# One of three weight subtractions of each expert moved from VectorE to GpSimd

## What is computed

```python
for e in range(E):
    a = _swiglu(xt @ expert_up_w[e].T)          # silu(gate half) * up half, I = 352
    out = out + cw[:, e:e + 1] * (a @ expert_down_w[e].T)
```

## Time and profile before

| | |
|---|---|
| time of the profiled execution | 2214.22 us |
| its span in the trace | 2212.1 us |
| TensorE busy, mean granted clock | 1779.5 us (80%), 0.901 |
| VectorE busy | 1611.7 us (73%) |
| ScalarE busy | 793.1 us (36%) |
| GpSimd busy | 1009.2 us (46%) |
| stage of the experts | from about 1700 us to the end |

### The profile page before, as it was taken

The page is one execution under the profiler, slowest core; times in us unless marked ns, Lnnn a source line. Parts: engine busy times, 40 slices in busy tenths (PEclk is TensorE's granted clock), DMA queues, the critical chain, the costliest instruction groups (busy, mean ns, idle before and its releaser), DMA issues. The chain is left out here.

```text
span 2212.1 us, 31372 instructions
## 1 busy us (share of the span) xinstructions
PE 1779.5 (80%) x8084; PEld 1285.4 (58%) x8084; DVE 1611.7 (73%) x2184; ACT 793.1 (36%) x1172; POOL 1009.2 (46%) x777
## 2 busy tenths in 40 slices
PE   3778767687676876768866668979997999999998
PEld 3345544454434554445543435657786999999997
DVE  0369999999989999899998834335763566655664
ACT  0444555445464553645545401211001233332332
POOL 1057547676576764767756532000001444433443
PEclk9989879798897997879978888999998999999999
DMA  5111101111101120011201042221121656666564
GB/s 135 69 29 64 53 25 35 39 58 56 29 30 40 54 64 24 30 40 49 69 25 30 24 162 85 95 106 57 58 79 44 163 124 165 162 146 164 143 161 82
DMA packets 81603, 169.61 MB, mean 77 GB/s; under 512 B 22459, under 2 KB 27467, under 8 KB 77979
## 3 DMA queue, kind: packets, MB, share of 16 engines
q1 hardware_dynamic: 57360, 116.06, 15.6%
q0 software_dynamic: 17856, 44.85, 10.4%
q10 hardware_dynamic: 6187, 6.37, 1.1%
HBM read 261.62 MB, written 39.24 MB: 136 GB/s over the span
## 5 line engine op out<-in xcount | busy, mean ns | idle before, releaser
L789 POOL TENSOR_TENSOR dbx<-u,b_all 128x512 f32<-128x512 f32 x512 | 642.2, 1278 | 350.5 <-DVE h L687 345.2
L687 DVE TENSOR_TENSOR_SCAN h<-da,dbx 128x512 f32<-128x512 f32 x512 | 596.2, 1203 | 40.2 <-ACT da L587 40.2
L587 ACT ACTIVATE da<-delta,a_neg 128x504 f32<-128x504 f32 x512 | 347.9, 684 | 474.1 <-DVE h L687 469.2
L427 PE MATMUL hT<-ident,h 128*128 128x128 f32 x2048 | 313.5, 313 | 229.6 <-DVE h L687 229.0
L427 PEld LDWEIGHTS hT<-ident,h 128*128 128x128 f32 x2048 | 274.8, 163 | 342.9 <-issue 337.6
L700 DVE SCALAR_TENSOR_TENSOR yacc<-hT,c_now,yacc 128x512 f32<-128x512 f32 x480 | 331.4, 732 | 4.3 <-PE hT L427 4.2
L334 PE MATMUL bank<-hid,w_in 128*128 128x512 f32 x608 | 291.4, 627 | 7.6 <-ACT hid L467 7.6
L1921 POOL DMA_INDIRECT out<-y,slots_kept x76 | 135.6, 1784 | 226.4 <-issue 158.1
L334 PEld LDWEIGHTS bank<-hid,w_in 128*128 128x128 f32 x608 | 120.4, 207 | 137.0 <-issue 128.1
L1554 POOL DMA_DIRECT2D slots_kept<-lists_kept x1 | 0.6, 577 | 331.2 <-DVE lists_kept L1508 331.2
L394 PE MATMUL bank<-w_out,skip 128*128 128x512 f32 x320 | 147.7, 609 | 2.5 <-DVE skip L659 2.5
(11 more groups left out here) (234 smaller groups left out, 3312.7 us busy)
## 6 DMA issues: line engine op xcount, KB each, us to landing
w_up_kept<-in_up_T SPq DMA_DIRECT2D x76, 1408.0 KB, 6.1
w_dn_kept<-in_dn_T SPq DMA_DIRECT2D x76, 768.0 KB, 7.4
b_all<-bt_scratch SPq DMA_DIRECT2D x128, 256.0 KB, 3.2
x_in<-in_x_pad ACTq DMA_DIRECT2D x21, 256.0 KB
res<-in_x_pad SPq DMA_DIRECT2D x20, 256.0 KB, 3.7
x_scratch<-res SPq DMA_DIRECT2D x20, 256.0 KB, 3.4
w_in<-in_in_T SPq DMA_DIRECT2D x8, 512.0 KB, 4.7
x_in<-x_scratch SPq DMA_DIRECT2D x4, 1024.0 KB, 5.3
```

Source lines behind the costliest of these rows:

```text
L427: mm = nc.tensor.transpose(hT[t][:, d * P:(d + 1) * P], h[:, m % RING, d, t * P:(t + 1) * P], ident[:])
L587: nc.scalar.activation(out[:, :, 1:], rows[:, :, 1:], ACT.Exp, scale=a_neg[:, d, n:n + 1]) \
L687: nc.vector.tensor_tensor_scan(h[:, n % RING, i, :], da[i % RING][:], dbx[:, i, :], 0.0, ALU.mult, ALU.add).then_inc(scan_done, 1)
L789: nc.gpsimd.tensor_tensor(dbx[:, i, :], u[:, d, :], b_all[:, m % RING, :], ALU.mult) \
```

## The change

The low part of the gate weights is no longer made by VectorE. A new function of GpSimd's program, `split_gate`, waits for `gate_split` and does the same subtraction of 128 x 1408 float32 numbers; it stands between the gather and the add of GpSimd's step i, when tile i starts a run. On VectorE the other two subtractions move up by one place each: `lower_up` takes the place of `lower_gate` ahead of `swiglu`, and `lower_down` the place of `lower_up` behind it; the extra look at the table for `lower_down` one step later goes away.

```diff
             first = weight_parts(dve, 0)
             x_out(0, 0)
-            lower_gate(first)
             lower_up(first)
             lower_down(first)
...
             with dve.If(run_starts):
-                lower_gate(parts)
+                lower_up(parts)
             swiglu(0, 0)
             with dve.If(run_starts):
-                lower_up(parts)
+                lower_down(parts)
...
                 x_out(i + 2, s)
-                started, of_started = starts(dve, i + 1), weight_parts(dve, i + 1)
-                with dve.If(started):
-                    lower_down(of_started)
                 with dve.If(run_starts):
-                    lower_gate(parts)
+                    lower_up(parts)
                 swiglu(i + 1, (r + 1) % RING)
                 with dve.If(run_starts):
-                    lower_up(parts)
+                    lower_down(parts)
...
+            def split_gate(i):
+
+                run = pool.value_load(table[0:1, 2, bass.ds(i, 1)], min_val=1, max_val=EXP)
+                slot = slot_of(run)
+                hi, lo = [part[:, slot, :, 0:INNER].rearrange("p o k f -> p (o k) f") for part in (w_up_hi, w_up_lo)]
+                pool.wait_ge(gate_split, run)
+                lo_part(nc.gpsimd, lo, w_up[:, :, 0:INNER], hi).then_inc(gate_ready, 1)
...
+            pool.sem_inc(gate_ready, 1)
...
                 gather(r % RING, ahead % LISTS, 16 * (j + loads), i + 1)
+                starts = pool.value_load(table[0:1, 1, bass.ds(i, 1)], min_val=0, max_val=1)
+                with pool.If(starts):
+                    split_gate(i)
                 add(i, r + TILES_AHEAD)
```

More of the change, by code:

```diff
@@ L1850, in a_out @@
                 less.then_inc(aT_out, 1)
[L1852 to L1855, removed]
             def lower_up(parts):
@@ L1872, in _ @@
             dve.sem_inc(aT_out, 1)
-            dve.sem_inc(gate_ready, 1)
             dve.sem_inc(up_ready, 1)
```

## The result

The changed kernel takes 2278.19 us (median of 4 runs, 2275.82 to 2281.9) against 2216.12 us (4 runs) of the kernel before: a ratio of 1.0279, 95% interval 1.0254 to 1.0303. The forecast was 2279 us. Over the later runs the kernel before has a median of 2216.89 us (28 runs, 2206 to 2225). The profiled execution of the changed kernel took 2278.81 us, with a span of 2276.7, 64.6 us more than before.

The account below looks back on a forecast made before the run. TensorE was taken to bound the experts' stage. Waits of 44.0 + 5 - 7.8 = 41 us plus 24 us of lowered clock made 65 us on 2214.22, so 2279 us; range 2230 to 2305 us.

Parts of the forecast that it names:

- What bounds the stage, and what could be won: Experts' stage: TensorE sets the time; all its waits after the stage's start, 7.8 us, are what relief for VectorE can return.
- The collision: Run starts: VectorE's up subtraction waits in full for GpSimd's, so swiglu and then TensorE come late, 2.9 us lost.
- When GpSimd can start: Run starts: GpSimd needs 1.2 us behind its gather for table and branch, bounds 0.3 and 1.83, starting at about 3.9.
- the second kind: 7 run starts with the gather ending at 3.4 to 4.7: VectorE goes first, go_up late, 2.4 us each, 16.8 us.
- The three kinds of starts: Experts' stage: the 15 run starts split into 6, 7 and 2 by when GpSimd's gather ends, together 44.0 us.
- the first kind: 6 run starts with the gather ending by 2.9: GpSimd goes first, 2.9 us lost each, 17.4 us.
- The first run: Start of the experts' stage: TensorE waits for GpSimd's gate part, 4.3 or 6.0 us later than before, taken as 5.
- The clock: Experts' stage: TensorE's standstills lower its granted clock 8.5 times at 2.8 us, 24 us, bounds 0 and 42.
- The clock doesn't stay: Judges the rival for the experts' stage that waits are the same but the clock stays: 2255 us, chance 0.18.
- Side by side: Rival at the run starts: GpSimd's and VectorE's subtractions run at the same time without hindrance; 2232 us, chance 0.10.
- GpSimd is last at every start: Rival at the run starts: slow table reading or growing lateness puts GpSimd behind VectorE each time; 2327 us, chance 0.12.
- the relief of VectorE could win: Rival in the experts' stage: moving lower_down wins 7.8 us and GpSimd's work is hidden; 2206 to 2210 us, chance 0.05.

Follow-up runs that it names:

- swiglu first: The changed kernel with VectorE's order at a run start turned to swiglu, then up part, then down part; 2227.12 us, ratio to before 1.0053.
- the run with filled standstills: The changed kernel with 14 extra matmuls on TensorE at each run start, ahead of the activation's transposes; 2252.08 us, ratio to before 1.0149.
- GpSimd relieved: The changed kernel with swiglu ahead of the up part and the down part one step later behind swiglu; 2227.22 us, ratio to before 1.0058.
- up part first: The changed kernel with GpSimd also waiting for VectorE's up part before it subtracts; 2290.89 us, ratio to before 1.0336.

## Why the prediction held, point by point

*What bounds the stage, and what could be won.* Right. TensorE without a wait takes 474.5 us; the waits were 7.6 to 7.8 us, all of them from the order on VectorE, and a version that moves one piece of VectorE's work takes them all back. The change's own move of the down part did too.

*The collision.* Right, and shown: VectorE's up part takes 3.39 us in the median beside a GpSimd subtraction, 1.63 beside a GpSimd instruction that only writes, 1.62 alone. It works in both directions: at tile 56 of the kernel with swiglu first, GpSimd's subtraction takes 4.20 us behind an up part that VectorE had begun 0.43 us before. That it reaches TensorE through `swiglu` was right as well: with `swiglu` ahead, 49 of the 56 us go.

*The price of the subtraction on GpSimd.* 3.2 us expected, 3.22 measured.

*When GpSimd can start.* Wrong. I took 1.2 us behind the gather for the table and the branch. At 12 of the 15 starts of the changed kernel the subtraction starts 0.25 us behind ScalarE's gate copy, so nothing of the table shows. Where the gather is what GpSimd waits for, it can start 0.02 us behind it (tile 41: gather to 3.52, subtraction from 3.54). At two starts there is more than either accounts for: at tile 15 it starts 0.81 us behind the gather and 0.46 behind the copy, at tile 56 0.19 and 0.41. With that, GpSimd is ready ahead of VectorE at many of the starts that I had put in the second kind.

*The three kinds of starts.* Wrong in their numbers: there was only the first kind, at all 15 starts. Besides the table's time, I had carried over GpSimd's lateness from the trace of before, but in the changed kernel the gather ended by 3.8 at all 15 starts, in place of up to 6.8. The sum was 44.0 us; what was measured is 40.2 us, as the 15 delays of the activation's transposes against 6.36 (9.04 on average), or 39.8 by the run with filled standstills. The two errors, dearer kinds and too many of them, came to 4 us only, since the kinds cost 2.4 and 4.9 us around the 2.9 of the first.

*The first run.* 5 us expected, 2.9 measured: GpSimd was ready at once there too, at 1712.3, 3.39 us behind the row transposes, and went ahead of both of VectorE's parts.

*The clock.* 24 us expected, 23.9 measured, but by other factors: it fell at 14 of the 15 starts, where I had 8.5, and a fall cost 1.7 us, where I had 2.8. That the two products agree is luck. The gaps were 2.1 to 3.0 us. I had counted on the scan stage, where gaps of 2.1 to 2.6 us lowered the clock half the time; here they did nearly always. And in the start at 2063 the clock was back by 2065.8 (the matmul spacing goes from 0.29 to 0.16 us there), while behind the gap at 1580 it took until 1589.

*The sum.* 65 us against 64.6 in the profiled execution looks closer than it is: 5.7 us of that are the launch's spread ahead of the stage, and the changed stage itself cost 58.8, that is 40.2 + 2.9 + 23.5 - 7.8. Against the median of before over all runs the difference is 61.3 us. The forecast was 6 us too high for the stage, and in the profiled execution the launch's spread happened to fill that up.

*The rivals.* The clock doesn't stay: the fill run would have shown no gain. Side by side is out by the stretched instructions. That GpSimd is last at every start didn't happen in the changed kernel, but forcing it gave the slowest kernel of all, 2290.89 us. That the relief of VectorE could win fails for a reason that I had named only in part: even with `swiglu` out of the collision's way (GpSimd relieved) the kernel is slower than before, since GpSimd's lateness behind its gathers becomes TensorE's.

What stays open: why a gap of 2.12 us at tile 5 of the changed kernel, and one of 2.31 us at tile 41 with GpSimd relieved, left the clock at full speed, while gaps of 2.12 us in the run with the up part first lowered it 15 times out of 15. No run here separates that.

## What to carry to other kernels

Before a piece of work moves to an idle engine, look for what that engine shares with the one relieved: here two subtractions that each fit took turns, one on GpSimd and one on VectorE with both operands in SBUF (`swiglu`, with one operand in PSUM, ran beside GpSimd's unharmed), and the one shut out keeps back what stands behind it in its program. Look at the order on the busy engine first: here all the waits that the move was to cure went away when one subtraction was put behind the instruction that TensorE waits for, and nothing moved. And count a long standstill of TensorE twice, once for itself and once for the clock: over the changed kernel and its variants, standstills of 2.1 to 3.0 us at the 15 starts behind the first run lowered it 30 times out of 32, those of up to 1.76 us never.

## What the runs showed of the hardware beyond that

- GpSimd's subtraction can start 0.02 us behind the end of the gather, table reads and branch included (tile 41 of the changed kernel; 0.00 to 0.03 us in most such places of the other kernels), and not the 0.85 to 1.83 us that VectorE and ScalarE showed between their instructions. At tile 56 it takes longer, 0.89 us with GpSimd relieved. Perhaps the reads are done while the gather is still running; only the times were measured.
- A memset of 3400 numbers on GpSimd (2.94 us) leaves VectorE's subtraction at 1626 ns, in contrast to a subtraction on GpSimd of about that length.
- The stages ahead of the experts end up to 6.5 us apart from launch to launch (1699.2 to 1705.7 us over ten profiles), which is as much as 0.3% of the kernel; comparing one stage's length was far sharper than comparing times.
